# Pooling score steps in the bank of the values product, and a new hand-written order of a batch on four engines

## What is computed

```
attn_in = tanh(x @ W1 + b1);  scores = attn_in @ v           # one score per token
p       = softmax(where(mask[kind], scores, -1e30))           # mask is l<=j, l>=j or l!=j, chosen by the batch's token
pooled  = (p @ x) / count(mask)
lat     = pooled @ w_kv_down;  k, v = lat @ w_kv_up;  q = pooled @ w_q      # 16 heads of 64
y       = causal_softmax(q k^T / 8) v;   x = x + y @ w_out
c       = x @ W[subject] + b[subject]
x       = x + bitlinear(gelu(bitlinear(c, w1)), w2)           # both with 8-bit quantised rows and ternary weights
```

## Time and profile before

| what | value |
|---|---|
| median of 3 runs (lowest to highest) | 1496.06 us (1492.96 to 1496.42) |
| the profiled execution, its own time | 1496.68 us |
| its span in the profile | 1495.1 us |
| TensorE (PE) busy in the span | 1310.1 us (88%) |
| VectorE (DVE), POOL, ScalarE (ACT) busy | 1156.1, 1116.0, 1011.0 us |
| mean granted TensorE clock | 0.952 |
| end of the tile loop, output product of batch 0, of batch 5 | 1057, 1148.5, 1400.2 us |

### The profile page before, as it was taken

The page is one execution under the profiler, slowest core; times in us unless marked ns, Lnnn a source line. Parts: engine busy times, 40 slices in busy tenths (PEclk is TensorE's granted clock), DMA queues, the critical chain, the costliest instruction groups (busy, mean ns, idle before and its releaser), DMA issues.

```text
span 1495.1 us, 20092 instructions
## 1 busy us (share of the span) xinstructions
PE 1310.1 (88%) x5491; PEld 732.1 (49%) x5492; DVE 1156.1 (77%) x1679; ACT 1011.0 (68%) x2388; POOL 1116.0 (75%) x685
## 2 busy tenths in 40 slices
PE   6688999989999999999998999799489889888984
PEld 2233443334334433343443568799355556555653
DVE  7599999999999999999999857555244555455554
ACT  3688878877887888788778772333166666666673
POOL 7599999999999999999999940444456556554551
PEclk8799999999999999999999999899699999999996
DMA  4544254334525442643354424312200000000000
GB/s 163 227 171 169 114 236 180 124 165 170 219 91 219 176 167 115 245 170 146 144 211 187 126 67 136 106 47 48 64 12 8 19 11 23 12 15 5 8 9 8
DMA packets 49123, 169.34 MB, mean 113 GB/s; under 512 B 15720, under 2 KB 33580, under 8 KB 40860
## 3 DMA queue, kind: packets, MB, share of 16 engines
q1 hardware_dynamic: 46780, 163.84, 28.6%
q0 software_dynamic: 2272, 4.66, 1.4%
HBM read 160.81 MB, written 7.67 MB: 113 GB/s over the span
## 4 chain that ended last, share of the span: by engine, by line
PE 46%; DVE 23%; ACT 16%; issue 12%; POOL 1%; DMA 1%; DVEq 0%; ACTq 0%; SPq 0%; POOLq 0%
DVE h L1227 12%; ACT banks L1192 8%; PE banks L1262 8%; DVE h L1208 5%; PE banks L399 4%; PE banks L723 3%; PE banks L782 3%; PE banks L761 2%; PE banks L408 2%; PE banks L797 2%; PE banks L700 2%; PE banks L663 2%; PE banks L1279 2%; PE banks L680 2%; PE banks L1113 2%
## 5 line engine op out<-in xcount | busy, mean ns | idle before, releaser
L1233 POOL TENSOR_TENSOR h<-h,Cb 128x1024 f32<-128x1024 f32 (+1 forms) x180 | 584.9, 3275 | 33.4 <-DVE h L1227 25.4
L1227 DVE TENSOR_TENSOR_SCAN h<-banks,h 128x1024 f32<-128x1024 f32 x256 | 573.7, 2274 | 20.1 <-ACT banks L1192 19.4
L1192 ACT ACTIVATE banks<-dt,A_cur 128x255 f32<-128x255 f32 x1024 | 422.6, 462 | 86.8 <-DVE h L1227 84.5
L1262 PE MATMUL banks<-h,ident 128*128 128x512 f32 x1024 | 467.9, 597 | 6.5 <-POOL h L1233 4.6
L1262 PEld LDWEIGHTS banks<-h,ident 128*128 128x128 f32 x1024 | 190.1, 190 | 250.6 <-issue 224.2
L1208 DVE TENSOR_TENSOR h<-Bb,banks 128x1024 f32<-128x1024 f32 (+1 forms) x131 | 204.5, 1562 | 2.9 <-DMA Bb<-scrX 2.0
L1214 POOL TENSOR_TENSOR h<-Bb,u 128x1024 f32<-128x1024 f32 x80 | 188.7, 2369 | 0.8 <-DMA Bb<-scrX 0.8
L753 POOL TENSOR_SCALAR h<-h 128x128 f32<-128x128 f32 (+1 forms) x128 | 101.5, 810 | 106.2 <-DVE h L746 106.1
L753 POOL TENSOR_SCALAR Cb<-Cb,h 128x128 f32<-128x128 f32 (+1 forms) x128 | 95.9, 767 | 53.9 <-DVE h L746 53.7
L1087 PE MATMUL banks<-xn,wF 128*128 128x512 f32 x256 | 117.2, 611 | 8.6 <-ACT xn L1079 8.6
L770 DVE COPY Bb<-banks 128x384 f32<-128x384 f32 x64 | 35.5, 554 | 75.3 <-PE banks L761 72.5
(11 more groups left out here) (292 smaller groups left out, 2079.5 us busy)
## 6 DMA issues: line engine op xcount, KB each, us to landing
Bb<-scrX SPq DMA_DIRECT2D x32, 2048.0 KB, 8.9
Cb<-scrX SPq DMA_DIRECT2D x32, 2048.0 KB, 9.8
h<-in_L_ffn_w SPq DMA_DIRECT2D x2, 2048.0 KB, 8.6
by_expert<-Cb SPq DMA_DIRECT2D x39, 64.0 KB, 1.5
h<-in_conv_w SPq DMA_DIRECT2D x4, 512.0 KB, 3.7
scr<-h SPq DMA_DIRECT2D x3, 640.0 KB, 3.0
wF<-scr SPq DMA_DIRECT2D x3, 512.0 KB
dt<-in_pmask SPq DMA_DIRECT2D x4, 257.0 KB, 2.9
```

Source lines behind the costliest of these rows:

```text
L1192: m = e.activation(ps_dA[c % 2][:, g, half, 1:S], dts[q][:, half, i * S + 1:(i + 1) * S], ACT.Exp, scale=A_cur[q][:, s:s + 1])
L1227: e.tensor_tensor_scan(chunk(i, c), ps_dA_flat[c % 2], chunk(i, c), 0.0, ALU.mult, ALU.add).then_inc(sem("scan"), 1)
L1233: e.tensor_tensor(h[i][:, rows(cs), :, :], h[i][:, rows(cs), :, :], both(Cb[i], cs), ALU.mult).then_inc(sem("hC"), len(cs))
L1262: m = e.matmul(bank(5), ident[:], h_flat[i][:, s * HALVES * S:(s + 1) * HALVES * S], start=(s == 0), stop=(s == NS - 1))
```

## The change

Two things change, both in the attention stage. The three pooling score steps (`x2t`, `at`, `S`) write to the second half of bank 4 in place of the first half of bank 5. Their waits for copies of `k`, and those of `k` for them, are gone; in their place stands a fence with the values product, which writes the first half of bank 4: `x2t` of batch k + 2 waits until `yturned` 3 of batch k has read the bank, `at` for number 4, `S` for number 5, and `values` 4, 5 and 6 wait for the copies of `x2t`, `at` and `S`. And the four texts that give the order of the pieces are new. No piece is added or taken away; the number of instructions of each kind stays.

```
--- before.py
+++ after.py
@@ -562,34 +562,36 @@
 
         def pe_x2t(e, b):
             e.wait_ge(sem("mo_acc"), 4 * b + 4)
-            wait(e, sem("ka_sb"), 2 * b - 1)
+            wait(e, sem("x2T"), 3 * b)
+            wait(e, sem("yTe"), 8 * (b - 2) + X2T_AFTER[0] + 1)
             for t in range(2):
-                m = e.transpose(bank(5)[:, t * P:(t + 1) * P], xt[:, 2 * b + t, :], ident[:])
+                m = e.transpose(bank(4)[:, S + t * P:S + (t + 1) * P], xt[:, 2 * b + t, :], ident[:])
             m.then_inc(sem("x2T_ps"), 1)
 
         def act_x2t(e, b):
             e.wait_ge(sem("x2T_ps"), 3 * b + 1)
-            e.activation(x2T, bank(5, S), ACT.Copy).then_inc(sem("x2T"), 1)
+            e.activation(x2T, bank(4)[:, S:2 * S], ACT.Copy).then_inc(sem("x2T"), 1)
 
         def pe_at(e, b):
             e.wait_ge(sem("x2T"), 3 * b + 1)
-            wait(e, sem("kv_sb"), 2 * b)
             if b == 0:
                 e.wait_ge(sem("pc_in"), 64)
-            e.matmul(bank(5, S)[0:32, :], cW1, x2T, start=True, stop=True).then_inc(sem("x2T_ps"), 1)
+            wait(e, sem("yTe"), 8 * (b - 2) + X2T_AFTER[1] + 1)
+            e.matmul(bank(4)[0:32, S:2 * S], cW1, x2T, start=True, stop=True).then_inc(sem("x2T_ps"), 1)
 
         def act_at(e, b):
             e.wait_ge(sem("x2T_ps"), 3 * b + 2)
-            e.activation(at_[0:32, :], bank(5, S)[0:32, :], ACT.Tanh, bias=cb1[0:32, :]).then_inc(sem("x2T"), 1)
+            e.activation(at_[0:32, :], bank(4)[0:32, S:2 * S], ACT.Tanh, bias=cb1[0:32, :]).then_inc(sem("x2T"), 1)
 
         def pe_S(e, b):
             e.wait_ge(sem("x2T"), 3 * b + 2)
-            e.matmul(bank(5, S), cv[0:32, :], at_[0:32, :], start=True, stop=True).then_inc(sem("x2T_ps"), 1)
+            wait(e, sem("yTe"), 8 * (b - 2) + X2T_AFTER[2] + 1)
+            e.matmul(bank(4)[:, S:2 * S], cv[0:32, :], at_[0:32, :], start=True, stop=True).then_inc(sem("x2T_ps"), 1)
 
         def act_S(e, b):
             e.wait_ge(sem("x2T_ps"), 3 * b + 3)
             wait(e, sem("pm"), b - 1)
-            e.activation(Sb[b % 2], bank(5, S), ACT.Copy).then_inc(sem("x2T"), 1)
+            e.activation(Sb[b % 2], bank(4)[:, S:2 * S], ACT.Copy).then_inc(sem("x2T"), 1)
 
         def gp_mask(e, b):
             wait(e, sem("pPT_ps"), b)
@@ -674,8 +676,6 @@
                 e.wait_ge(sem("lat"), b + 1)
             else:
                 e.wait_ge(sem("ka_sb" if c == 2 else "kv_sb"), 2 * b + (c + 1) // 2)
-            if c > 1 and b + 1 < B:
-                e.wait_ge(sem("x2T"), 3 * b + (4 if c == 2 else 6))
             for i in range(2):
                 m = e.matmul(fold(bank(5), 2)[:, i, :], Wk[:, (2 * c + i) * P:(2 * c + i + 1) * P], latT,
                              start=True, stop=True)
@@ -775,6 +775,8 @@
             e.wait_ge(sem("PTv"), 8 * b + p + 1)
             e.wait_ge(sem("PTa"), 8 * b + p + 1)
             wait(e, sem("yTe"), 8 * b + p)
+            if p - 1 in X2T_AFTER and b + 2 < B:
+                e.wait_ge(sem("x2T"), 3 * b + 7 + X2T_AFTER.index(p - 1))
             for kc in range(2):
                 q0, n = ((0, 2 * P), (P, P))[kc]
                 for o in range(2):
@@ -1886,35 +1888,23 @@
 
 
 
+X2T_AFTER = (3, 4, 5)
 ATT_GP = """
-norm:2 norm:3 gather:0 norm:4 norm:5 gather:1 norm:6 norm:7 norm:n0 norm:n1 mask"""
+gather:l1 gather:0 norm:4 norm:5 norm:6 norm:7 norm:n0 mask norm:n1 norm:n2 norm:n3"""
 ATT_PE = """
-turn:0 score:3 turn:1 V:2 values:l7 V:3
-turn:2 score:4 turn:3 pturn values:0 o2
-turn:4 score:5 pool turn:5 fx values:1
-turn:6 lat score:6 turn:7 q:0 fc values:2 k:0
-turn:8 score:7 q:1 turn:9 fqturn k:1 values:3 fu:0 fu:1
-turn:10 x2t score:n0 turn:11 q:2 values:4 k:2
-turn:12 at score:n1 turn:13 q:3 values:5
-turn:14 S score:n2 turn:15 v:0 k:3 fq2turn values:6 v:1 fd"""
+score:3 v:l1 turn:0 V:2 turn:1 values:l7 score:4 turn:2 V:3 o2 turn:3 values:0 pturn fx score:5 pool turn:4 values:1
+fc score:6 turn:5 lat turn:6 values:2 q:0 turn:7 score:7 k:0 fqturn q:1 fu:0 turn:8 values:3 fu:1 turn:9 score:n0
+x2t turn:10 q:2 turn:11 k:1 values:4 turn:12 score:n1 q:3 turn:13 at k:2 values:5 turn:14 score:n2 fq2turn k:3
+turn:15 S v:0 values:6 fd"""
 ATT_ACT = """
-prob:4 prob:5 turned:1 yturned:l7 pexp V:2 V:3
-prob:6 prob:7 turned:3 yturned:0 pturned
-prob:8 prob:9 turned:5 yturned:1 fx
-prob:10 lat prob:11 turned:7 q:0 yturned:2
-prob:12 q:1 prob:13 turned:9 fqturned k:1 yturned:3 fg:0 fg:1
-prob:14 prob:15 turned:11 x2t q:2 yturned:4
-prob:n0 prob:n1 turned:13 at q:3 yturned:5
-prob:n2 prob:n3 turned:15 S yturned:6 k:3 v:0 v:1"""
+prob:6 pexp turned:1 V:3 prob:7 pturned yturned:0 turned:3 prob:8 fx prob:9 yturned:1 prob:10 turned:5 prob:11 lat
+yturned:2 q:0 prob:12 prob:13 fqturned turned:7 q:1 fg:0 yturned:3 fg:1 turned:9 x2t prob:14 prob:15 q:2 turned:11
+yturned:4 k:1 prob:n0 at prob:n1 prob:n2 yturned:5 turned:13 q:3 k:3 S v:0 turned:15 prob:n3 prob:n4 yturned:6 v:1
+V:n2 yturned:7 prob:n5"""
 ATT_DVE = """
-turned:0 tt:6 tt:7 inv:2 pmax
-turned:2 tt:8 pnorm tt:9 inv:3
-turned:4 tt:10 x3 tt:11 inv:4 pool
-turned:6 tt:12 fc tt:13 inv:5 fq k:0
-turned:8 tt:14 tt:15 inv:6 comb
-turned:10 tt:n0 tt:n1 inv:7 fq2:0
-turned:12 k:2 tt:n2 fq2:1 tt:n3 inv:n0 fq2:2
-turned:14 tt:n4 fq2turned tt:n5 inv:n1 fo"""
+pmax inv:2 turned:2 pnorm tt:8 inv:3 tt:9 x3 tt:10 tt:11 turned:4 inv:4 fc pool tt:12 tt:13 fq tt:14 inv:5 turned:6
+k:0 tt:15 turned:8 inv:6 tt:n0 turned:10 fq2:0 tt:n1 fq2:1 turned:12 inv:7 tt:n2 tt:n3 fq2:2 k:2 inv:n0 fq2turned
+tt:n4 tt:n5 turned:14 fo tt:n6 comb inv:n1 tt:n7 turned:n0"""
 
 
 PE_ORDER = """
```

## The result

The changed kernel took **1445.7 us** (median of four, 1444.06 to 1448.70) beside 1496.24 for the kernel before: ratio 0.9664, 95% interval 0.9636 to 0.9692. The forecast was 1437.3 in 1427 to 1456. Measured three times more in the course of the experiments, the same kernel came out at 1436.2, 1445.0 and 1436.8, with ratios of 0.9573, 0.9648 and 0.9601. So what stands fast is a gain of 3.4 to 4.3%, and there is a spread of 9 us to explain too.

The account below looks back on a forecast made before the run. TensorE was taken as the bound, with five named stalls and a clock loss per full batch. Ramp -10, five full batches -43.2 and end -5.6 sum to -58.8: 1496.68 becomes 1437.9, or 1437.3 for the median, range 1427 to 1456 us.

Parts of the forecast that it names:

- A full batch: Five full attention batches, one `o2` to the next: 50.34 us falls to 41.7, bounds 41.2 to 44.
- the 0.3 added: Allowance of 0.3 us a full batch for three places with under 0.2 us in hand.
- The clock: TensorE's granted clock in full batches should stay at 1.00, 2.4 GHz, with waits that short.
- The fences: Bank 4 waits between score steps and values products: all met in time, by 0.2 to 2 us.
- Rival C: ScalarE's Gelu table switches each cost a second 1.28 us: 15 us more, 1453 us; chance 0.02.
- The ramp: From the tile loop's end to batch 0's `o2`: 10 us shorter, bounds 6 to 13.
- the term of the two indirect DMAs: First `mask` in the ramp behind ten indirect DMAs instead of 12, some 1.2 us each: up to 2.3 us earlier.
- The end: Batch of 42.54 us becomes 39.9 (-2.6), batch of 30.11 becomes 27 (-3), tail of 22.3 unchanged.
- A: Whole kernel runs as laid out, each stall's cause removed: 1428 to 1446 us; chance 0.70.
- Rival B: TensorE waits 1 to 3 us more a batch where slack is small, clock falls sometimes: 1446 to 1461; chance 0.20.
- D: Fences stop TensorE at `x2t`, `at`, `S`, up to 5.5 us each: slower, about 1530 us; chance 0.04.
- E: A loop over the four queues limits, not TensorE; stalls only move: no difference, 1496 us; chance 0.04.

Follow-up runs that it names:

- its two Gelu edits: Changed kernel with ScalarE's copy `yturned` 3 moved behind both Gelus (1447.2 us) or ahead of both (1451.3 us), beside 1445.0 us unedited.
- both edits meant for it: Changed kernel with a normalisation between the gather pairs (1433.6, 1434.6 us), or SyncE's conditioned-weights load later (1436.2, 1435.9 us).

## Why the prediction was right

- **A full batch: 41.7 us forecast, 40.87 measured**, in all ten batches of the two undisturbed repeats and in the two undisturbed ones of the first profile. The terms: 0.2 us of wait at `x2t`, measured 0.2, from the same releaser; the 0.3 added for `turned` 5, `q` 2 and values 6 were not needed, no such wait exists; the work was taken as 41.2, the middle of 40.9 from the pieces and 41.5 from the busy time, and 40.61 was measured. So the sum of the pieces was the better of the two. Of the other, read in steps of 2 us, the old batch has a clock below 1.00 only from 1224.95 to 1232.95 (0.67, 0.50, 0.50, 0.63); that slowed its busy time by 3.0 us and not 2.7, which leaves 41.2. Where the last 0.6 us went stays open. This made the forecast 5 x 0.83 = 4.2 us too high.
- **The clock** stayed at 1.00 in every full batch without a stall, as put.
- **The fences**: `at`, `S` and values 4 to 6 have no wait at all in the full batches of the new order, as laid out (ScalarE's queue has 52 pieces, not the 43 that were counted, but the same ones as before). That they can bite is shown by the bank alone (2.7 us).
- **No table load more, and no drain.** Loads 8 and 7, each 1283 ns, and Exp starts at 1296.40, 0.02 us after the load ends. Rival C is dead. The trace agrees with the load's figure in the Trainium skill (ScalarE: Activation LUTs, What ACT_TABLE_LOAD costs) and shows nothing of its 1380 ns for a drain at a switch.
- **The ramp: -10 forecast**, -9.3 in the first profile and -10.1 in the last. The first mask starts 12.47 us after the first gather instead of 14.74, 2.3 earlier, which is the term of the two indirect DMAs. The first values product starts 44.9 us after the first gather, 49.1 before: 4.2 of gain forecast at 5.0. But the prediction gave the whole to the layout and did not say which piece of it; the runs show that 6.4 us hang on POOL's order, and both of the waits that are longer with the old one go back to the second mask.
- **The end**: 39.9 forecast, 39.3 measured; 27 forecast, 27.5 to 27.6 undisturbed, 29.45 in the first profile, where TensorE's clock was 0.88 instead of 0.94 and its waits for `turned` the same 2.9 us; the tail 0 forecast, 0 measured.
- **What no term had**: 2.0, 1.8 and 2.0 us of stall in the first three batches, with the clock's fall in two of them (2.08 + 3.78 + 3.70 = 9.6 us in all), and 3.0 us of later start. Without these two the first profile stands at 1448.7 - 12.6 = 1436.1, 1.8 under the 1437.9 forecast for a profiled execution. The two undisturbed repeats (1436.16 and 1434.65 us, starts 2.7 and 1.1 later than before the change) stand at 1433.4 and 1433.6 by the same reckoning, 4.4 under the forecast, of which the full batches are 4.2. The first profile has 2.6 us more than these, from 0.8 in the ramp and 1.9 in the batch of 30.11.
- **Luck in the number**: the 1445.7 us lies in the range, and only just in that of A (1428 to 1446), because two misses work against each other: the full batches without a stall gained 4.2 us more than forecast, while the stall, which stood in no term and no rival, took 9.6 in the profile. The mechanism is shown by the waits and the batch time and not by the total. (The terms given for the lower end of the range make 1428.7 and not 1427, with 3 us in them that no term names; nothing hangs on it.)
- **Rival B** said that TensorE would wait 1 to 3 us more a batch where the slack is small, and that the clock would fall now and then. By size the first measurement is nearly B (1446 to 1461), by mechanism it is not: the wait stands where ScalarE and VectorE stop as well, not where the layout was tight, and B's slip of ScalarE's queue at the Gelu was tried (the copy behind both Gelus) and costs 0.5 us.
- **Rivals D and E** fell with the sign. Of E something is true where the bank stays shared: with the order alone, waits of 3.8 us a batch remain, of which 3.5 are at that bank.

## What to carry to other kernels

When the bound engine has small waits with known causes, lay out its queue without waits and place the other queues under it piece by piece: here this gave the batch to within 0.3 us (40.9 of work and 0.2 of wait laid out, 40.87 measured with that wait in it), better than the busy time taken from the profile (41.5). Moving a resource without moving the order only moves the wait, and a new order without the resource fails at the old wait; cost them as one. And cost the ramp by itself, where a piece with ample time in the steady state may be what everything waits for.

## What the chip did that I had not expected

- ScalarE and VectorE, and behind them TensorE, stand still for about 2 us at one place of a batch, on some executions and chips and not on others, in the three full batches in which four indirect DMAs and SyncE's loads fall together. The profile names no releaser. It was seen in the first measurement's profile and in all four profiles of one chip (2.0, 0.9, 2.0 us in the changed kernel), in none of eight profiles of another, four of them with the very four gathers in a row and the loads beside or behind them. The stalling chip was used on one occasion only, so chip and occasion can't be told apart. Whether gathers, loads or something else is behind it was not settled: both edits meant for it ran only where it does not occur.
- The length of a wait alone does not give its price. 0.8 and 0.9 us cost 0.5 and 0.9 us more than the 0.2 before, at clock 1.00. Of the twelve stalls of 0.9 to 2.3 us in the changed kernel and its two Gelu edits, nine cost their own length within 0.1 us (even those of 2.3), and three, of 1.8 to 2.0 us, cost 3.7 to 3.8, with a mean clock of 0.96 in the batch. A wait of 2.6, in the order alone, was followed by some 3 us at 0.50, the lower of the clock's two levels (1.2 of 2.4 GHz).
- The changed kernel differs by 8 to 9 us (0.6%) between measurements on two chips, while the kernel before differs by less than 5 (1496.2 to 1501.1), and by 4.3 of these on one and the same chip. So a gain of this size should be given with the chip's own run of the kernel before, and here it is 3.4 to 4.3%.
